# Running sums of the softmax in one stretch on GpSimd, with one probability tile buffer for each of the eight key tiles

## The reference, cut to what matters

```
q, k, v = x @ wq.T, x @ wk.T, x @ wv.T         # 16 heads of 128
q = rope(rmsnorm(q) * q_norm_w);  k = rope(rmsnorm(k) * k_norm_w)
s = 50 * tanh(q @ k.T / sqrt(128) / 50)        # 1024 x 1024 for each head and batch
p = softmax(where(key > query, -inf, s))
y = (p @ v) @ wo.T;  x = layernorm(x + y)
```

## Time and profile before

| | |
|---|---|
| median of 3 runs | 1169.97 us (1167.75 to 1170.66) |
| profiled execution, its own time | 1168.05 us |
| its span in the trace | 1166.3 us |
| PE busy | 1030.0 us, 88% |
| DVE busy | 922.7 us, 79% |
| POOL busy | 788.6 us, 68% |
| ACT busy | 684.7 us, 59% |
| mean granted clock of TensorE | 0.953 of full |

### The profile page before, as it was taken

The page is one execution under the profiler, slowest core; times in us unless marked ns, Lnnn a source line. Parts: engine busy times, 40 slices in busy tenths (PEclk is TensorE's granted clock), DMA queues, the critical chain, the costliest instruction groups (busy, mean ns, idle before and its releaser), DMA issues.

```text
span 1166.3 us, 19884 instructions
## 1 busy us (share of the span) xinstructions
PE 1030.0 (88%) x6256; PEld 821.3 (70%) x6256; DVE 922.7 (79%) x1356; ACT 684.7 (59%) x1095; POOL 788.6 (68%) x699
## 2 busy tenths in 40 slices
PE   4799999999999999999999999999999869859910
PEld 3578888888888888878787878787878745335500
DVE  3499999999999999999989899999999885413206
ACT  2476666666666666767676767676767724202303
POOL 1488787878787878787777777777878742262322
PEclk9899999999999999999999999999999989969955
DMA  8110101000001000000000000000000039239435
GB/s 320 46 38 19 38 21 33 23 32 23 32 23 32 23 32 27 27 27 27 27 27 27 27 27 27 27 27 27 27 27 19 19 89 274 54 105 234 86 56 187
DMA packets 49306, 65.97 MB, mean 57 GB/s; under 512 B 10528, under 2 KB 41216, under 8 KB 48768
## 3 DMA queue, kind: packets, MB, share of 16 engines
q1 hardware_dynamic: 43184, 58.55, 16.2%
q0 software_dynamic: 3072, 4.46, 2.2%
q10 hardware_dynamic: 3024, 2.64, 0.7%
HBM read 54.35 MB, written 11.29 MB: 56 GB/s over the span
## 4 chain that ended last, share of the span: by engine, by line
PE 39%; DVE 28%; issue 15%; DMA 9%; ACT 5%; POOL 2%; DVEq 1%; SPq 1%; another core or an unknown queue 0%; ACTq 0%; POOLq 0%
PE ps L357 11%; PE ps L359 10%; PE ps L358 10%; DMA acc_rows<-ye,acci 6%; DVE prob_lo L987 6%; DVE yacc L1063 5%; DVE vS_lo L987 3%; PE ps L385 3%; DVE qhat_hi L997 2%; ACT prob_hi L666 2%; PE ps L391 2%; DVE qhat_lo L987 2%; DVE qraw L1040 2%; PE ps L529 2%; DVE wo_hi L997 1%
## 5 line engine op out<-in xcount | busy, mean ns | idle before, releaser
L987 DVE TENSOR_TENSOR prob_lo<-praw,prob_hi 128x1024 fp32r<-128x1024 f32 (+7 forms) x256 | 370.1, 1474 | 7.3 <-ACT prob_hi L666 7.0
L872 POOL TENSOR_TENSOR pacc<-pacc,praw 128x768 f32<-128x768 f32 (+2 forms) x192 | 268.0, 1396 | 12.8 <-POOL praw L857 9.2
L666 ACT ACTIVATE prob_hi<-praw 128x1024 fp32r<-128x1024 f32 (+7 forms) x256 | 170.8, 681 | 148.5 <-POOL praw L857 147.0
L857 POOL TENSOR_SCALAR_AFFINE_SELECT praw<-praw 128x128 f32<-128x128 f32 x256 | 136.4, 544 | 159.6 <-ACT praw L705 159.6
L699 ACT ACTIVATE praw<-ps,rstd 128x1024 f32<-128x1024 f32 (+7 forms) x256 | 188.2, 736 | 85.0 <-PE ps L359 46.2
L705 ACT ACTIVATE praw<-praw 128x1024 f32<-128x1024 f32 (+7 forms) x256 | 165.6, 672 | 0.0
L357 PE MATMUL ps<-qhat_hi,kT_hi 128*128 128x512 f32 (+3 forms) x384 | 138.6, 361 | 16.6 <-DVE qhat_lo L987 15.7
L357 PE MATMUL ps<-prob_hi,vS_hi 128*128 128x512 f32 (+3 forms) x384 | 136.7, 356 | 4.9 <-DVE prob_lo L987 4.9
L358 PE MATMUL ps<-qhat_lo,kT_hi 128*128 128x512 f32 (+3 forms) x384 | 133.3, 347 | 0.0
L358 PE MATMUL ps<-prob_lo,vS_hi 128*128 128x512 f32 (+3 forms) x384 | 133.3, 347 | 0.0
L359 PE MATMUL ps<-qhat_hi,kT_lo 128*128 128x512 f32 (+3 forms) x384 | 133.2, 347 | 0.0
(11 more groups left out here) (149 smaller groups left out, 2033.4 us busy)
## 6 DMA issues: line engine op xcount, KB each, us to landing
rqB<-rq_rows SPq DMA_DIRECT2D x32, 512.0 KB, 3.7
wgu<-in_wgu SPq DMA_DIRECT2D x16, 704.0 KB
wd<-in_wd SPq DMA_DIRECT2D x16, 352.0 KB
wraw<-in_wqkv SPq DMA_DIRECT2D x16, 256.0 KB, 3.6
acc_rows<-pacc SPq DMA_DIRECT2D x4, 1024.0 KB, 13.4
wv<-in_wqkv SPq DMA_DIRECT2D x16, 128.0 KB, 2.0
woraw<-in_wo SPq DMA_DIRECT2D x16, 128.0 KB, 2.0
yacc<-in_x SPq DMA_DIRECT2D x1, 2048.0 KB, 14.2
```

What stands on the lines that cost most here:

```text
L666: return nc.scalar.activation(dst, src, ACT.Copy)
L857: nc.gpsimd.affine_select(out=diag, in_=diag, compare_op=ALU.is_ge, fill=0.0, base=0, pattern=[[1, P]], channel_multiplier=-1).then_inc(ma ...
L872: nc.gpsimd.tensor_tensor(pacc[:, b, P * j:T], before, raw, ALU.add).then_inc(pacc_done, 1)
L987: v.tensor_tensor(dst, x_, hi.bitcast(F32), ALU.subtract).then_inc(done, 1)
```

## The change

`RING` becomes 8, and the buffers are sized exactly: tile j has 1024 - 128 j columns at its own place in `praw` and `prob`; tile 0 of `praw` alone exists twice, for b = 0 and 1. `pacc` becomes a single row for both. To make room, `rqB` shares its memory with `qsq`, `sumT` with `sqT`, and `gtmp` with a piece of `praw`; waits are added for these overlays. On GpSimd the adds of a step move out from between its masks into the next step. There the order is: masks 6 and 7 of s-1, the square, adds 0 to 7 of s-1, masks 0 and 1, the power for q, masks 2 and 3, the power for k, masks 4 and 5. On TensorE `sums` moves from ahead of `sums_of_squares` to behind scores 3; on VectorE `summed` moves behind the fold of squares and the weight split, and `UNIT_ORDER` follows. The zeroed memory is written in nine transfers of 1024 columns instead of five of 2048.

```diff
-RING = 4
+RING = TT
+COLS = [T - P * j for j in range(TT)]
+AT = [sum(COLS[:j]) for j in range(TT)]
+def raw_at(b, j):
+    at = AT[j] if j or not b else sum(COLS)
+    return slice(at, at + COLS[j])
...
-UNIT_ORDER = "q0 q1 k0 k1 sums ss op0 op1 v0 op2 op3 v1".split()
+UNIT_ORDER = "q0 q1 k0 k1 ss sums op0 op1 v0 op2 op3 v1".split()
...
-        praw = asb("praw", [P, RING, T])
-        prob = pair("prob", [P, RING, T])
-        pacc = asb("pacc", [P, B, T])
+        praw = asb("praw", [P, sum(COLS) + T])
+        prob = pair("prob", [P, sum(COLS)])
+        pacc = asb("pacc", [P, T])
...
+        rqB = qsq
...
-        sumT = asb("sumT", [P, 32 * TT])
+        sumT = sqT[:, 0:32 * TT]
...
-            for c0 in range(0, 2 * ACCR // P * D, 2 * T):
+            for c0 in range(0, 2 * ACCR // P * D, T):
...   (TensorE, step)
-                    sums(s - 1, 1 - b, *hd.unit(b, "sums"))
                 if new:
                     sums_of_squares(s + 1, *hd.unit(b, "ss"))
                 scores(s, b, 2)
                 scores(s, b, 3)
                 if old:
+                    sums(s - 1, 1 - b, *hd.unit(b, "sums"))
...   (ScalarE, tanh)
-                act.wait_ge(pacc_done, t + (2 if j == RING else 1))
+                if j:
+                    act.wait_ge(pacc_done, t + 1)
+                elif not (isinstance(s, int) and s == 0):
+                    act.wait_ge(pacc_done, t + 2 - TT)
...   (GpSimd, square_queries and accumulate)
-                    pool.wait_ge(folded, step)
+                    pool.wait_ge(qf_done, step)
...
+                if j == 0 and not (isinstance(s, int) and s == 0):
+                    pool.wait_ge(rsum_done, s)
...   (GpSimd, step)
-                    mask(s - 1, 6)
-                    mask(s - 1, 7)
-                    accumulate(s - 1, 1 - b, 6)
-                    accumulate(s - 1, 1 - b, 7)
+                    mask(s - 1, 1 - b, 6)
+                    mask(s - 1, 1 - b, 7)
                 if new:
                     square_queries(s + 1, hd.unit(b, "q1")[0])
+                if old:
+                    for j in range(TT):
+                        accumulate(s - 1, 1 - b, j)
+                if new:
                     if b == 1:
                         next_head_weight(h, s)
-                mask(s, 0)
-                mask(s, 1)
+                mask(s, b, 0)
+                mask(s, b, 1)
                 if new:
                     rms_queries(1 - b, hd.unit(b, "ss")[0])
-                accumulate(s, b, 0)
-                accumulate(s, b, 1)
...
-                accumulate(s, b, 2)
...
-                accumulate(s, b, 3)
-                mask(s, 4)
-                accumulate(s, b, 4)
-                mask(s, 5)
-                accumulate(s, b, 5)
+                mask(s, b, 4)
+                mask(s, b, 5)
...   (VectorE, the fold of squares; summed)
+                    if not isinstance(step, int) or step > 2:
+                        dve.wait_ge(rsum_done, step - 2)
...
+                dve.wait_ge(pj_free, count - 1)
...   (VectorE, step)
                     output_lo(s - 1)
-                    summed(1 - b, *hd.unit(b, "sums"))
                 if new:
                     projected("ss", 1 - b, s + 1, *hd.unit(b, "ss"))
                     if b == 0 and not hd.last:
                         split_next_weights(hd)
                 if old:
+                    summed(1 - b, *hd.unit(b, "sums"))
                     out_projected(1 - b, 0, s - 1, *hd.unit(b, "op0"))
```

More of the change, by code:

```diff
@@ L428, in sums @@
                 pe.wait_ge(pacc_done, (s + 1) * TT + RING)
-                strip_sums(bank_no, 0, strips(pacc[:, b, :])).then_inc(pj_done, 1)
+                strip_sums(bank_no, 0, strips(pacc[:, :])).then_inc(pj_done, 1)
             def out_proj(s, b, u, count, bank_no):
@@ L763, in _ @@
             s = B * H
-            hi(s - 1, 7)
+            hi(s - 1, 1, 7)
             output_hi(s - 1)
@@ L821, in _ @@
             nc.gpsimd.memset(ident[:, :], 0.0).then_inc(consts, 1)
-            nc.gpsimd.memset(pacc[:, :, :], 0.0).then_inc(zeros_set, 1)
+            nc.gpsimd.memset(pacc[:, :], 0.0).then_inc(zeros_set, 1)
             pool.wait_ge(consts, 3)
@@ L862, in accumulate @@
                 t = s * TT + j
+                if j == 0 and not (isinstance(s, int) and s == 0):
+                    pool.wait_ge(rsum_done, s)
                 pool.wait_ge(mask_done, t + 1)
-                raw = praw[:, j % RING, 0:T - P * j]
+                raw = praw[:, raw_at(b, j)]
                 if j == 0:
                     pool.sem_inc(waited, 1)
-                    nc.gpsimd.tensor_copy(pacc[:, b, 0:P], raw[:, 0:P]).then_inc(pacc_done, 1)
+                    nc.gpsimd.tensor_copy(pacc[:, 0:P], raw[:, 0:P]).then_inc(pacc_done, 1)
                 else:
-                    before = praw[:, 0, P:T] if j == 1 else pacc[:, b, P * j:T]
+                    before = praw[:, raw_at(b, 0)][:, P:T] if j == 1 else pacc[:, P * j:T]
                     pool.wait_ge(pacc_done, t + RING)
-                    nc.gpsimd.tensor_tensor(pacc[:, b, P * j:T], before, raw, ALU.add).then_inc(pacc_done, 1)
+                    nc.gpsimd.tensor_tensor(pacc[:, P * j:T], before, raw, ALU.add).then_inc(pacc_done, 1)
             def next_head_weight(h, s):
@@ L918, in _ @@
             for j in (6, 7):
-                mask(B * H - 1, j)
-            for j in (6, 7):
+                mask(B * H - 1, 1, j)
+            for j in range(TT):
                 accumulate(B * H - 1, 1, j)
@@ L1098, in step @@
                 if old:
-                    tile(s - 1, 4)
-                    tile(s - 1, 5)
-                    tile(s - 1, 6)
+                    tile(s - 1, 1 - b, 4)
+                    tile(s - 1, 1 - b, 5)
+                    tile(s - 1, 1 - b, 6)
                 if old:
-                    tile(s - 1, 7)
+                    tile(s - 1, 1 - b, 7)
                 if new:
@@ L1114, in step @@
                 if old:
+                    summed(1 - b, *hd.unit(b, "sums"))
                     out_projected(1 - b, 0, s - 1, *hd.unit(b, "op0"))
-                tile(s, 0)
+                tile(s, b, 0)
                 if old:
                     out_projected(1 - b, 1, s - 1, *hd.unit(b, "op1"))
-                tile(s, 1)
+                tile(s, b, 1)
                 if new:
@@ L1123, in step @@
                     out_projected(1 - b, 2, s - 1, *hd.unit(b, "op2"))
-                tile(s, 2)
+                tile(s, b, 2)
                 if old:
@@ L1130, in step @@
                     scale_raw(s + 1)
-                tile(s, 3)
+                tile(s, b, 3)
                 if new:
@@ L1175, in _ @@
             for n, j in enumerate((4, 5, 6, 7)):
-                tile(s - 1, j)
+                tile(s - 1, 1, j)
                 tile_stats(TT * n // 4, TT * (n + 1) // 4)
```

65 lines of the change are left out of this document (32 added, 33 removed).

## The result

The changed kernel takes 1246.15 us (median of 4 runs, 1240.04 to 1250.07), the kernel before 1169.88 beside it: a ratio of 1.065 (95% interval 1.0601 to 1.0700), slower. The forecast was 1306, its range 1240 to 1335. The profiled execution took 1250.07 us, 82.0 more than the one of before.

A forecast was written before the change was run, and what follows sets the result against it. TensorE, busy 55.15 of 56.60 us, was taken as the bound. 1168.05 + 127.5 (thirty steps at 4.25) + 9 (first step, last step, tail) = 1304.6; with 1.9 for the shown runs' median, 1306, range 1240 to 1335.

The forecast's parts named there:

- the stretch: GpSimd's square and eight running sums before masks 0 and 1, ending at C + 14.35 in the mean, bounds 11.5 and 17.
- C: Zero of the step's clock: the end of VectorE's second copy of the next q.
- VectorE in the way: VectorE's two-input work on tiles 4 to 7 during GpSimd's square and adds, charged to GpSimd at +1.3 us.
- the stall: TensorE, at the column sums by C + 10.9, stands until the last add: 3.6 us a step.
- rival (a): TensorE stalls at the sums but its clock holds: 30 x 2.6 us, total 1257; chance 0.19.
- The clock term: TensorE at half clock after standing at the sums: 1.65 us a step, bounds 0 and 3.3.
- From the sums to the next q1: TensorE's part of a step: sums 0.5, then 15.1 us to the next q1, plus 1.65 for the clock.
- The rest of the sum: Outside the thirty middle steps: first step -2, step 31 +5, last step and tail +6; together +9 us.
- Rival (b): Broadcast of q's norm comes late behind masks 0 and 1: 1 us a step, 30 more, 1336; chance 0.08.
- Rival (d): GpSimd's square and adds take 11.5 to 12.5 us, TensorE's clock holds: 1172 to 1202; chance 0.06.
- rival (c): Faster: VectorE freed of blocks, TensorE never stands and runs at 27.6 us a step: 1155; chance 0.04.
- the false floor: TensorE's busy time taken as 27.6 us a step, leaving at most 0.7 us a step to win.

The follow-up runs named there:

- Experiment 3: Changed kernel with adds 2 to 7 cut to 32 columns, so the running sums leave out most of those tiles: 1122.37 us, 0.9609 of the kernel before.
- experiment 7: Changed kernel with GpSimd computing the square of q twice, the second over the first: 1345.91 us, 1.1504 of the kernel before.
- experiment 1: Changed kernel's exact buffers and overlays kept, order of all engines put back to the kernel before: 1179.21 us, 1.0103 of the kernel before.
- experiment 2: Changed kernel with eight extra matmuls, results overwritten, ahead of TensorE's wait for the column sums: 1204.43 us, 1.0306 of the kernel before.
- experiment 6: Changed kernel with the square of q moved from GpSimd to ScalarE ahead of tanh 0, all work done: 1129.36 us, 0.9650 of the kernel before.
- experiment 9: Kernel before with adds 2 to 7 cut to 32 columns, order and ring of four kept: 1125.65 us, 0.9643 of the kernel before.
- experiment 8: Kernel before with only the square of q moved from GpSimd to ScalarE: 1177.52 us, 1.0092 of the unedited kernel before.

## Why the prediction was right or wrong

**The direction and the main mechanism were right.** TensorE waits for `pacc` in every step, the squares are further apart, the clock is under 1.00, tile 1 takes 1.08 us, ScalarE's wait for masks is mostly gone. Experiment 3 shows that it is the length of the stretch, and not the order or a wait by itself; experiment 7 shows that the path takes any addition to it whole; experiment 1 shows that, but for 1%, it isn't the buffers. Not separated is what the late masks of tiles 0 and 1 would cost if TensorE didn't wait: they end 0.5 us behind the last add.

**The stretch was sized too long: this is the main error of the number.** It was put at C + 14.35 in the mean, and is C + 13.0: from C = 404.32 the last add ends at 417.52 (with weights to split), and in the next step from 435.39 at 448.21. The term that was mis-sized is the one for VectorE in the way, 1.3 us for tiles 4 to 7: what VectorE has with two inputs in the stretch was added to GpSimd's time. It was VectorE that stood (tile 5 took 2.50 us, tile 7 2.21), and GpSimd's adds took what they take by themselves: 2.18, 1.86, 1.56, 1.30 and 1.00 us for 2.13, 1.83, 1.56, 1.29 and 1.01. Without weights to split, GpSimd's work was put at 12.6 us undisturbed and 13.9 with VectorE; it took 12.8. The other terms cancel nearly: the gap between dependent adds is 0.08 and not 0.15, and the split of the next weights costs 0.4 and not 0.9, but the square and its start took 2.5 for 2.25 and the copy 0.62 for 0.29. (By the prediction's own slope tiles 4 to 6 alone are 0.67, 0.54 and 0.40 us, not 0.55, 0.45 and 0.35; they measure 0.68, 0.55 and 0.41.) TensorE asks at C + 10.7, forecast C + 10.9. So the stall is 2.35 us in the mean and not 3.6: some 1.3 us a step, or 40 of the 54.5 us by which the 1304.6 lie above the profiled 1250.07.

**That the time falls into the range is partly luck.** It lies 6 us above the lower end. The part of the range that belongs to the forecast's own mechanism began at 1281; below that it was there for rival (a), which is wrong.

**The clock term was right.** It was 1.65 us a step, with bounds of 0 and 3.3; experiment 2 gives 1.52. Rival (a), in which the clock holds, was wrong, though its total was near: 1257 against 1246.15. It had the stall too long and the clock's price at nothing, and these cancel. Without experiment 2 the measured time would have spoken for it.

**From the sums to the next q1:** 417.57 to 434.50 = 16.9 us, forecast 0.5 + 15.1 + 1.65 = 17.25. Right.

**The rest of the sum:** first part -7.3 where -2 was said; thirtieth middle step, last step and tail together +12.9 where 4.25 + 11 was. Rival (b), the late broadcast, was not seen: its transfers landed after 3.8 us, and VectorE has no wait for them. Rival (d) had the right shape (a shorter stretch) but took the clock to hold.

**Wrong: what bounds the kernel before.** "TensorE is the bound; it leaves at most 0.7 us a step" is false. A change can win 1.34 us a step (28.30 - 26.96): experiments 3, 6 and 9 are 3.5 to 4% faster, and experiment 6 does so with all the work done. The step that failed is the reading of the earlier trace rows: 55.15 of 56.60 us busy was taken for work. Busy time of pipelined matmuls also covers as much of each delay as two records overlap; the same matmuls need 53.92 when nothing holds them up. And rival (c) named the mechanism that most likely makes up that loss, VectorE blocked by adds, but the false floor capped it at 21 us. It didn't change the outcome, as the condition of (c), a stretch within C + 10.9, failed as forecast. It would have pointed at the better kernel: the same order, with the square taken out of the stretch.

**Left open:** the 1% of the exact buffers; why experiment 8 loses a little (in both the tile of 896 columns takes some 2.59 us in every step, and in the kernel before only in every second); the part of VectorE and of GpSimd's queue in what held the kernel before; what the late masks cost by themselves; and how much of the 2.4 us between C + 8.3 and C + 10.7 in experiment 6 could still be filled.

## What to carry to other kernels

Before work is gathered into an idle gap of an engine, add up its length against the moment at which the next engine asks for the last of it, and let it start before the event that opens the gap if it doesn't need that event: here 13.0 us against 10.7 lost 6.5%, and 8.3 against 10.7, with the square on another engine, won 3.5%. Don't take the busy share of a pipelined engine for its floor; look instead for instructions of one shape whose mean differs from the shortest of their kind, as they show who is held up (not yet what it costs: experiment 8 freed some of it and won nothing). If a short stall recurs in every step, price the clock after it separately.

## What the runs showed of the hardware

- A stall of 2.1 to 2.7 us once per step was enough for the clock to fall in 29 of 30 steps. The clock cost 1.52 us a step on top of the 2.45 of the stall itself. Eight useless matmuls in it made the kernel 41.7 us faster.
- The square on ScalarE took 2.20 us, twice the 1.02 to 1.11 of its other instructions on 128x1024 values. It reads and writes in a transposing order there; whether that is why was not tried. The step of experiment 6 is at 26.96 us all the same.
- The copy of 128x128 on GpSimd took 0.62 us behind the square in the kernel after and 0.29 in the kernel before, in experiment 6, and in the last step of the kernel after, where no square stands before it. Why was not tested.
- Not every pair of instructions of GpSimd and VectorE meets. In the kernel before GpSimd's power on 128x8 values ran from 446.39 for 1.85 us, and VectorE's subtraction of 128x512 with two inputs in SBUF began at 446.77 beside it and took its usual 0.69 us.
